# Low part of the rotated keys: from GpSimd at the end of a group to VectorE at the end of the next group's first quad

## The chip, the core and the metric

One core of one Trainium2 chip. The metric is the device time of one execution, in microseconds. A core has TensorE (matrix products into PSUM), VectorE, ScalarE and GpSimd (elementwise work), and queues that issue DMA transfers. VectorE and ScalarE can read PSUM. Each engine runs its own list of instructions in order; semaphores tie the lists together.

## What is computed

Input x is 8 batches of 512 tokens of 256 channels. The output is x + attention(layernorm(x)) + experts(layernorm(x)). The mixture of 16 experts is done before the part that matters here. The attention has 16 heads of 64 channels, with rotated queries and keys and a bias by distance:

```
qkv = (x @ qkv_w.T).reshape(B, S, 3, H, D)
q, k = rope(q, c, s), rope(k, c, s)      # (t1*c - t2*s, t1*s + t2*c)
scores = einsum('bhqd,bhkd->bhqk', q, k) / 8
kb = -p * log1p(a * abs(i - j))
out = einsum('bhqk,bhkd->bhqd', softmax(scores + kb), v)
return out.reshape(B, S, H*D) @ out_w.T
```

## The kernel before

Products of float32 values are made from float16 pairs: a value is split into a high part (its float16 rounding) and a low part (value minus high part, in float16), and each product is three TensorE passes (high-high, high-low, low-high; the list PARTS).

**Stages.** `prepare` (layer norm, routing, tables) and `experts` run first; `attention` takes over at about 280 us of the profile. It has 8 batches of 4 groups; a group is 4 heads of one batch, numbered g = 4b + j. A group has 4 quads, each 128 query rows of all 4 heads; quad n belongs to group n // 4. `over_quads` walks the 128 quads on every engine.

**One quad on TensorE** (`quad`, line 1631): scores (L1572, into four banks ps_s), the transposes of the previous quad's probabilities of two heads (L1585, into ps_t), a fill, the value products of quad n-2 (L1607, first from pt_pe, then from pt_dma), another fill. **Fills** are projections for later groups and the output projection, all through the one PSUM bank ps_x: per group in the order qk0, v0, qk1, v1, qk2, qk3, y0, y1, two to a quad (POSITIONS, line 1026). A fill waits until the one before has been read (`x_free`). The projections (L1528 for q and k, L1538 for v) are for the group F two ahead (`ahead`); the last two groups of batch 7 have none.

**One quad on VectorE** (`quad`, line 1447): read the second fill of the quad before, then `negate` for three heads (L1424: scores scaled plus bias, and their minimum), read this quad's first fill, `negate` for the fourth head, on odd quads `read_context`, and `pair_low` (L1430, low part of the transposed probabilities, out of ps_t). A fill of q or k is read by L1390 (times the cosine and sine table, into prods), one of v by L1374 after ScalarE's L1249. Each of these reads at most one input from SBUF, the other from PSUM.

**ScalarE** does the exponentials (L1286), the high parts (`turned_high` L1270, `prob_high` L1276, `high` L1265 for the rotated queries and keys, at the end of the second and fourth quad of a group), and some copies.

**GpSimd**, per group (`group`, line 1193), in this order: prob_low of the first quad (L1163: low part of the two heads' probabilities that go through a DMA transpose), rotate the queries of F (L1153: sum of products, into rot), ctx_parts (L1171), prob_low of the second quad, multiply (L1143), low part of the rotated queries (`low(F, 0)`, L1157), prob_low of the third, rotate the keys (`rotate(F, 1)`), prob_low of the fourth, **low part of the rotated keys (`low(F, 1)`, L1157)**, ctx_parts, and at the end in batches 0 to 6 either two gathers of expert rows for the next batch (j < 2, L1179, indirect DMAs) or `combine` (j >= 2: L1189 and L1191, which weigh these rows and add them to the residual). The first rotation of the next group waits for the low part of the keys by `parts_lo` >= 2F and by `x_free`.

**The DMA queue** (`turn_probs`) issues the transpose of prob_parts into pt_dma once `prob_lo` of that quad is signalled; the values of that quad wait for it two quads later.

`parts` is a ring of five (high, low) tiles: entry 2F for the queries and 2F + 1 for the keys of group F. The scores of a group wait in their first quad for `parts_lo` >= 2F + 2.

Of the kernel before, what the change touches and what calls it, by code (L numbers as in the profile page):

```python
# [18 lines left out]
ALU = mybir.AluOpType  # L19
# [7 lines left out]
E, F, C = 16, 1024, 256  # L27
TOK = NB * S
NT = TOK // P
TPB = S // P  # L30
KT = M // P
NG, HG = 4, 4
# [947 lines left out]
def attention(nc, sem, ctx, x, out, xt_dram, xcur, x_loaded, o_sb, o_stored, expert_dram, source_dram, gate_dram, ident,  # L980
# [8 lines left out]
    def sb(name, shape, dt=F32):  # L989
        return ctx.enter_context(nc.sbuf_tensor(name, shape, dt))  # L990
# [3 lines left out]
    rot = sb("rot", [P, 2, S])  # L994
    parts = sb("parts", [P, 5, 2, 2, S], F16)
# [53 lines left out]
    parts_hi, parts_lo = sem("parts_hi"), sem("parts_lo")  # L1049
# [9 lines left out]
    def fills_before(b, l):  # L1059

        n = 2 * FILLS + PAIRS * b + l
        n = n - (min(max(l - 6, 0), 2) if b == 0 else 2)
        if b == NB - 1:
            n -= sum(m // 8 >= 2 and m % 8 < FILLS for m in range(l))
        return n
# [5 lines left out]
    def wait(eng, s, v):  # L1071

        if v > 0:
            eng.wait_ge(s, v)

    def ahead(b, j):

        return None if b == NB - 1 and j >= 2 else 4 * b + j + 2
# [59 lines left out]
    def on_gpsimd(pool):  # L1138
        def multiply(F, fills):

            pool.wait_ge(x_free, fills)
            pool.wait_ge(rotated, 2 * F)
            nc.gpsimd.tensor_tensor(prods[:, 0:2, :], proj[:].unsqueeze(1).to_broadcast([P, 2, S]), trig[:, 1:3, :],  # L1143
                                    ALU.mult).then_inc(multiplied, 1)

        def rotate(F, w, fills):

            pool.wait_ge(x_free, fills)
            if w and F >= 2:
                pool.wait_ge(multiplied, F - 1)  # L1150
            pool.wait_ge(parts_lo, 2 * F + w)
            p = prods1 if (F, w) == (1, 1) else prods
            nc.gpsimd.tensor_tensor(rot[:], p[:, 0:2, :], p[:, 2:4, :], ALU.add).then_inc(rotated, 1)  # L1153

        def low(F, w):
            pool.wait_ge(parts_hi, 2 * F + w + 1)
            nc.gpsimd.tensor_tensor(parts[:, (2 * F + w) % 5, 1], rot[:], parts[:, (2 * F + w) % 5, 0], ALU.subtract).then_inc(parts_lo, 1)  # L1157

        def prob_low(n):
            if n < 0 or n == LAST:  # L1160
                return
            pool.wait_ge(prob_hi, n + 1)
            nc.gpsimd.tensor_tensor(prob_parts[:, n % 2, 1], prob[:, (2 * n + 1) % 3], prob_parts[:, n % 2, 0],  # L1163
                                    ALU.subtract).then_inc(prob_lo, 1)

        def context_lo(unit):
            if unit < 0 or unit >= LAST_UNIT - 1:
                return
            two = slice(2 * (unit % 2), 2 * (unit % 2) + 2)
            pool.wait_ge(ctx_hi, unit + 1)  # L1170
            nc.gpsimd.tensor_tensor(ctx_parts[:, 1, two].rearrange("p t c -> p (t c)"), ctxt[:],  # L1171
                                    ctx_parts[:, 0, two].rearrange("p t c -> p (t c)"), ALU.subtract).then_inc(ctx_lo, 1)

        def gather(b, half):

            pool.wait_ge(routes_loaded, 32 * b + 32)
            wait(pool, combined, 2 * b + half - 1)
            for i in range(2 * half, 2 * half + 2):
                nc.gpsimd.indirect_dma_start(  # L1179
                    got[:, i, :], None, expert_dram[:, :],  # L1180
                    bass.IndirectOffsetOnAxis(ap=source[:, i:i + 1], axis=0),
                    bounds_check=E * C - 1, oob_is_err=False).then_inc(gathered[half], 16)

        def combine(b, half):

            pool.wait_ge(gathered[half], 32 * b + 32)
            pool.wait_ge(residual_loaded, 16 * b + 16)
            two = slice(2 * half, 2 * half + 2)
            nc.gpsimd.tensor_tensor(got[:, two, :], got[:, two, :], gate[:, two].unsqueeze(2).to_broadcast([P, 2, M]), ALU.mult).then_inc(weighted, 1)  # L1189
            pool.wait_ge(weighted, 2 * b + half + 1)  # L1190
            nc.gpsimd.tensor_tensor(res[:, two, :], res[:, two, :], got[:, two, :], ALU.add).then_inc(combined, 1)  # L1191

        def group(b, j):
            g = NG * b + j
            F = ahead(b, j)
            prob_low(4 * g)
            if g == 0:
                rotate(1, 1, FIRST_FILLS.index((1, "qk", 3)) + 1)
                combine(0, 0)
                low(1, 1)  # L1200
                combine(0, 1)
            if F:
                rotate(F, 0, fills_before(b, 8 * j) + 3)
            context_lo(2 * g - 1)
            prob_low(4 * g + 1)
            if F:
                multiply(F, fills_before(b, 8 * j) + 5)
            if F:
                low(F, 0)
            prob_low(4 * g + 2)  # L1210
            if F:
                rotate(F, 1, fills_before(b, 8 * j) + 6)
            prob_low(4 * g + 3)
            if F:
                low(F, 1)
            context_lo(2 * g)
            if b < NB - 1:
                if j < 2:
                    gather(b + 1, j)
                else:  # L1220
                    combine(b + 1, j - 2)

        def rotate_queries():

            pool.wait_ge(x_free, 2)
            nc.gpsimd.tensor_tensor(prods0[0][:, 0:2, :], prods0[0][:, 0:2, :], prods0[0][:, 2:4, :], ALU.add).then_inc(rotated, 1)

        rotate_queries()
        for r in range(2):
            pool.wait_ge(o_stored[r], 16 * (E // 2))  # L1230
        gather(0, 0)
        rotate(1, 0, FIRST_FILLS.index((1, "qk", 1)) + 1)
        gather(0, 1)
        low(1, 0)
        for b in range(NB):
            for j in range(NG):
                group(b, j)
# [132 lines left out]
    def on_vector(dve):  # L1370
# [33 lines left out]
        def read_fill(b, l):  # L1404
            kind = fill_at(b, l)
            if kind and kind[0] == "v":
                read_val(kind[2], kind[1])
            elif kind and kind[0] == "qk" and kind[1] != 2:
                dve.wait_ge(filled, fills_before(b, l) + 1)
                read_q(kind[2], kind[1], prods)  # L1410
            elif kind and kind[0] == "y":
                read_y(b, l, kind[1], fills_before(b, l))
# [15 lines left out]
        def pair_low(n):  # L1428
            dve.wait_ge(turned_hi, n + 1)
            nc.vector.scalar_tensor_tensor(out=pt_pe[:, n % 2, 1].rearrange("p q k c -> p q (k c)"), in0=ps_t[:],  # L1430
                                           scalar=P_SCALE, in1=pt_pe[:, n % 2, 0].rearrange("p q k c -> p q (k c)"),
                                           op0=ALU.mult, op1=ALU.subtract).then_inc(turned_lo, 1)

        def read_context(unit):

            dve.wait_ge(pv_done, 4 * unit + 4)
            dve.wait_ge(sums_scaled, unit + 1)
            nc.vector.reciprocal(rsum[:], sums[:, unit % 2].rearrange("p n u -> p (n u)")).then_inc(chain, 1)
            dve.wait_ge(chain, unit + 1)
            if unit == LAST_UNIT:  # L1440
                dve.wait_ge(end_turned, 1)
            else:
                wait(dve, ctx_lo, unit)
            nc.vector.tensor_tensor(ctxt[:].rearrange("p (i d) -> p i d", d=D), ps_o[:].rearrange("p (i d) -> p i d", d=D),
                                    rsum[:].unsqueeze(2).to_broadcast([P, 8, D]), ALU.mult).then_inc(ctx_read, 1)

        def quad(n, b, q):
            j, t = divmod(q, TPB)
            if q:
                read_fill(b, 2 * q - 1)  # L1450
            elif b:
                read_fill(b - 1, PAIRS - 1)
            negate(n, j, t, 0)
            negate(n, j, t, 1)
            negate(n, j, t, 2)
            if n:
                read_fill(b, 2 * q)
            negate(n, j, t, 3)
            if n == 0:
                read_val(0, 1)  # L1460
                read_val(1, 0)
                read_val(1, 1)
                read_q(1, 2, prods1)
                read_q(1, 3, prods1)
                read_fill(b, 2 * q)
            if n % 2 and n >= 3:
                read_context(n // 2 - 1)
            if n:
                pair_low(n - 1)

        def first_low(w):
            dve.wait_ge(parts_hi, w + 1)
# [217 lines left out]
```

## Time and profile before

| | |
|---|---|
| Time, median of three runs | 1146.76 us (1145.97 to 1149.74) |
| Profiled execution | 1150.09 us |
| its span | 1148.4 us |
| TensorE busy | 1064.0 us (93%) |
| ScalarE busy | 1021.2 us (89%) |
| VectorE busy | 1005.8 us (88%) |
| GpSimd busy | 826.6 us (72%) |
| Granted TensorE clock, mean | 0.97 |
| Shares of the chain that ended last | PE 65%, ACT 9%, DMA 8%, DVE 7%, POOL 6%, issue 4% |

The chain is the path of work and waits followed back from the last instruction. PE is TensorE, PEld its weight loads, DVE VectorE, ACT ScalarE, POOL GpSimd. L1157 is line 1157 of the kernel. "Idle before" is the idle time of an engine ahead of an instruction, with what ended it. Instructions of one engine overlap a little at their ends, so that an instruction that waits for nothing starts about 0.08 us before the recorded end of the one ahead of it.

### The profile page before, as it was taken

The page shows a single profiled execution, that of the slowest core. Times are in us where ns is not written, and L with a number is a line of the kernel's source. Part 1 is how long each engine was busy: PE and PEld are TensorE (multiplying, and loading weights), DVE is VectorE, ACT ScalarE, POOL GpSimd, SP SyncE. Part 2 cuts the span into 40 slices and gives each one's busy share as a digit, 9 for nine tenths or more (in the row PEclk, how much of TensorE's full clock was granted, in tenths as well). Part 3 has the DMA queues.
Part 4 walks back from the last instruction along what each step waited for, and adds up shares of the span by engine and source line. Part 5 has one row for each costly group of instructions (what it writes and reads, how often), then busy time and mean ns, then how long its engine had stood idle before and what let it go on. Part 6 is the DMA issues. An engine that isn't in the chain of part 4 may idle for free.

```text
span 1148.4 us, 35585 instructions
## 1 busy us (share of the span) xinstructions
PE 1064.0 (93%) x14470; PEld 776.9 (68%) x14470; DVE 1005.8 (88%) x2050; ACT 1021.2 (89%) x2013; POOL 826.6 (72%) x483
## 2 busy tenths in 40 slices
PE   3547999999799999999999999999999999999977
PEld 2436988887466676676766666767667676776756
DVE  8788999996688999999989888999999988899976
ACT  3797999984589999999999999999999999999985
POOL 5471010002699999899999899989999999999842
PEclk9667999999999999999999999999999999999999
DMA  8885676751148557766766685585667557855564
GB/s 292 311 264 189 208 265 220 240 202 52 33 82 157 113 95 148 130 99 107 167 98 107 130 153 106 95 155 124 101 119 153 112 103 135 153 94 111 112 112 92
DMA packets 383106, 164.75 MB, mean 143 GB/s; under 512 B 336610, under 2 KB 372463, under 8 KB 382944
## 3 DMA queue, kind: packets, MB, share of 16 engines
q1 hardware_dynamic: 368832, 137.98, 57.2%
q0 software_dynamic: 5440, 16.61, 3.9%
q10 hardware_dynamic: 8672, 7.90, 2.3%
q8 instruction: 114, 1.87, 0.7%
q14 instruction: 48, 0.39, 0.1%
HBM read 58.79 MB, written 21.00 MB: 69 GB/s over the span
## 4 chain that ended last, share of the span: by engine, by line
PE 65%; ACT 9%; DMA 8%; DVE 7%; POOL 6%; issue 4%; SPq 0%; POOLq 0%; ACTq 0%; DVEq 0%
PE ps_o L1607 12%; PE ps_s L1572 11%; PE ps_x L1528 10%; PE ps_t L1585 8%; PE ps_x L1547 6%; PE ps_x L1538 6%; PE psh L941 5%; PE pso L956 5%; DMA pt_dma<-prob_parts 4%; ACT prob L1286 2%; DMA ot<-ctx_parts 2%; DVE wlo L874 2%; POOL prob_parts L1163 2%; POOL parts L1157 1%; DMA xt_dram<-xth 1%
## 5 line engine op out<-in xcount | busy, mean ns | idle before, releaser
L1286 ACT ACTIVATE prob<-prob,neg_max 128x512 f32<-128x512 f32 x512 | 365.2, 715 | 4.7 <-DVE neg_max L1424 2.6
L1424 DVE CUSTOM_DVE_ANT_0 prob<-ps_s,strips,score_scale 128x512 f32<-128x512 f32 x512 | 360.4, 746 | 10.3 <-PE ps_s L1572 5.9
L1163 POOL TENSOR_TENSOR prob_parts<-prob,prob_parts 128x1024 f16<-128x1024 f32 x127 | 272.1, 2143 | 78.4 <-ACT prob_parts L1276 78.1
L1572 PE MATMUL ps_s<-parts 32*128 32x512 f16 x3072 | 191.2, 379 | 1.1 <-DVE parts L1473 1.0
L1430 DVE SCALAR_TENSOR_TENSOR pt_pe<-ps_t,pt_pe 128x1024 f16<-128x1024 f32 x128 | 156.0, 1219 | 36.2 <-ACT pt_pe L1270 36.1
L1585 PEld LDWEIGHTS ps_t<-ident,prob 128*128 128x128 f32 x1024 | 110.7, 142 | 58.2 <-issue 38.6
L1153 POOL TENSOR_TENSOR rot<-prods 128x1024 f32<-128x1024 f32 x61 | 144.3, 2365 | 3.2 <-DVE prods L1390 3.2
L1528 PE MATMUL ps_x<-xcur,wqkv_hi 128*128 128x512 f16 x480 | 143.7, 381 | 2.2 <-DVE pt_dma L1390 1.3
L1585 PE MATMUL ps_t<-ident,prob 128*128 128x128 f32 x1024 | 140.7, 281 | 3.8 <-DVE pt_pe L1430 3.8
L771 POOL DMA_DIRECT2D expert_dram<-xa x16 | 17.9, 1120 | 173.1 <-ACT xa L816 173.1
L1276 ACT CAST prob_parts<-prob 128x1024 f16<-128x1024 f32 x127 | 132.9, 1046 | 4.0
L1270 ACT ACTIVATE pt_pe<-ps_t 128x1024 f16<-128x1024 f32 x128 | 130.7, 1021 | 3.8 <-PE ps_t L1585 3.5
L1157 POOL TENSOR_TENSOR parts<-rot,parts 128x1024 f16<-128x1024 f32 x62 | 132.9, 2143 | 0.4 <-ACT parts L1265 0.4
L1572 PEld LDWEIGHTS ps_s<-parts 32*128 32x128 f16 x3072 | 68.9, 93 | 92.5 <-issue 33.4
L1390 DVE TENSOR_TENSOR prods<-ps_x,trig 128x1024 f32<-128x1024 f32 x90 | 110.0, 1222 | 15.8 <-PE ps_x L1528 15.6
L1607 PE MATMUL ps_o<-val_hi,pt_dma 128*128 128x64 f16 x2048 | 111.6, 194 | 11.8 <-DMA pt_dma<-prob_parts 11.7
L1607 PEld LDWEIGHTS ps_o<-val_hi,pt_pe 128*128 128x128 f16 x2048 | 104.0, 98 | 11.0 <-issue 0.3
L1607 PE MATMUL ps_o<-val_hi,pt_pe 128*128 128x64 f16 x2048 | 111.1, 193 | 0.0
L1607 PEld LDWEIGHTS ps_o<-val_hi,pt_dma 128*128 128x128 f16 x2048 | 99.4, 98 | 13.2 <-DMA pt_dma<-prob_parts 6.9
L1607 PE MATMUL ps_o<-val_lo,pt_dma 128*128 128x64 f16 x1024 | 104.1, 194 | 0.0
L1607 PE MATMUL ps_o<-val_lo,pt_pe 128*128 128x64 f16 x1024 | 103.7, 193 | 0.0
L1607 PEld LDWEIGHTS ps_o<-val_lo,pt_pe 128*128 128x128 f16 x1024 | 91.2, 98 | 11.0 <-issue 0.3
(219 smaller groups left out, 2599.4 us busy)
## 6 DMA issues: line engine op xcount, KB each, us to landing
raw<-in_L_ffn_w_dram SPq DMA_DIRECT2D x32, 1024.0 KB, 6.2
xa<-in_L_attn_x_dram SPq DMA_DIRECT2D x8, 512.0 KB, 9.1
slots_dram<-zeros POOLq DMA_DIRECT2D x4, 1024.0 KB, 8.9
xt_dram<-xth SPq DMA_DIRECT2D x8, 512.0 KB, 6.5
xa<-slots_dram SPq DMA_DIRECT2D x16, 256.0 KB, 5.3
expert_dram<-xa POOLq DMA_DIRECT2D x16, 256.0 KB, 5.0
xcur<-xt_dram SPq DMA_DIRECT2D x8, 512.0 KB, 4.8
res<-in_L_attn_x_dram ACTq DMA_DIRECT2D x8, 512.0 KB, 4.1
```

The source lines that it names most:

```text
L1153: nc.gpsimd.tensor_tensor(rot[:], p[:, 0:2, :], p[:, 2:4, :], ALU.add).then_inc(rotated, 1)
L1157: nc.gpsimd.tensor_tensor(parts[:, (2 * F + w) % 5, 1], rot[:], parts[:, (2 * F + w) % 5, 0], ALU.subtract).then_inc(parts_lo, 1)
L1163: nc.gpsimd.tensor_tensor(prob_parts[:, n % 2, 1], prob[:, (2 * n + 1) % 3], prob_parts[:, n % 2, 0], ALU.subtract).then_inc(prob_lo, 1)
L1270: nc.scalar.activation(pt_pe[:, n % 2, 0].rearrange("p q k c -> p q (k c)"), ps_t[:], ACT.Copy, scale=P_SCALE).then_inc(turned_hi, 1)
L1276: nc.scalar.copy(prob_parts[:, n % 2, 0], prob[:, (2 * n + 1) % 3]).then_inc(prob_hi, 1)
L1286: nc.scalar.activation(prob[:, s % 3, q, :], prob[:, s % 3, q, :], ACT.Exp, bias=neg_max[:, 2 * (s % 3) + q:2 * (s % 3) + q + 1], scale=-1 ...
L1424: nc.vector.tensor_tensor_reduce(prob[:, s % 3, q, :], ps_s[u][:], strips[:, HG * j + u, start:start + S], score_scale[:, 0:1], 3.0e38, AL ...
L1430: nc.vector.scalar_tensor_tensor(out=pt_pe[:, n % 2, 1].rearrange("p q k c -> p q (k c)"), in0=ps_t[:], scalar=P_SCALE, in1=pt_pe[:, n % 2 ...
L1528: last = nc.tensor.matmul(bank, wt[a][:, kt, c:c + P], xcur[:, x, kt, :], start=(m == 0), stop=(m == 3 * KT - 1))
L1572: last = nc.tensor.matmul(ps_s[h][:], parts[rows, 2 * F % 5, a, f, t * P:(t + 1) * P], parts[rows, (2 * F + 1) % 5, c, f, :], start=(i == ...
L1585: last = nc.tensor.transpose(ps_t[:, q, kt * P:(kt + 1) * P], prob[:, 2 * n % 3, q, kt * P:(kt + 1) * P], ident[:])
L1607: last = nc.tensor.matmul(ps_o[:, c:c + D], pt[:, n % 2, x, q, kt, :], val[a][:, g, kt, u * D:(u + 1) * D], start=(m == 0), stop=(m == 3 * ...
```

## The change

VectorE gets a function `key_low` with the subtraction that GpSimd's `low(F, 1)` did, with the same operands and semaphores, and runs it at the end of the first quad of each group from the second on (after `pair_low`), for the F of the group before. GpSimd no longer does it in `group`; it still does `low(F, 0)`, and `low(1, 1)` once at the start. 30 operations move, of the groups 0 to 29.

```
@@ group, on GpSimd
             prob_low(4 * g + 3)
-            if F:
-                low(F, 1)
             context_lo(2 * g)
@@ on_vector
+        def key_low(F):
+            dve.wait_ge(parts_hi, 2 * F + 2)
+            nc.vector.tensor_tensor(parts[:, (2 * F + 1) % 5, 1], rot[:], parts[:, (2 * F + 1) % 5, 0], ALU.subtract).then_inc(parts_lo, 1)
@@ quad, on VectorE
             if n:
                 pair_low(n - 1)
+            if n and t == 0 and ahead(*divmod(n // TPB - 1, NG)):
+                key_low(ahead(*divmod(n // TPB - 1, NG)))
```

## Rows read from the trace of the kernel before

**Rows 1.** The page's first part: busy time, share of the span, instructions.
```profile
PE 1064.0 (93%) x14470; PEld 776.9 (68%) x14470; DVE 1005.8 (88%) x2050; ACT 1021.2 (89%) x2013; POOL 826.6 (72%) x483
```
**Rows 2.** Stretch 320 to 1100 us: length, busy time per engine, clock, DMA share, GB/s.
```profile
320.00:1100.00 780.00, 770.83 (x11671) 538.77 (x11668) 702.10 (x1405) 740.98 (x1588) 714.43 (x386) 1.00 0.66 121
```
**Rows 3.** Waits from 320 to 1100 us: total, times, longest.
```profile
POOL prob_parts L1163 <- ACT prob_parts L1276: 54.7, 62, 2.5
...
PE ps_o L1607 <- DMA pt_dma<-prob_parts: 6.0, 10, 1.4
```
**Rows 4.** Timeline of VectorE, quads 64 to 66: start, us, operation, idle before.
```profile
726.58 1.22 DVE L1430 SCALAR_TENSOR_TENSOR pt_pe<-ps_t,pt_pe 128x1024 f16<-128x1024 f32 x1
728.25 0.69 DVE L1374 TENSOR_TENSOR val_lo<-ps_x,val_hi 128x512 f16<-128x512 f32 x1 [0.45 <-ACT val_hi L1249]
728.97 0.75 DVE L1424 CUSTOM_DVE_ANT_0 prob<-ps_s,strips,score_scale 128x512 f32<-128x512 f32 x1
...
730.32 0.75 DVE L1424 CUSTOM_DVE_ANT_0 prob<-ps_s,strips,score_scale 128x512 f32<-128x512 f32 x1
...
731.29 1.23 DVE L1390 TENSOR_TENSOR prods<-ps_x,trig 128x1024 f32<-128x1024 f32 x1 [0.22 <-PE ps_x L1528]
...
733.94 1.22 DVE L1430 SCALAR_TENSOR_TENSOR pt_pe<-ps_t,pt_pe 128x1024 f16<-128x1024 f32 x1
735.07 0.68 DVE L1374 TENSOR_TENSOR val_lo<-ps_x,val_hi 128x512 f16<-128x512 f32 x1
735.67 0.74 DVE L1424 CUSTOM_DVE_ANT_0 prob<-ps_s,strips,score_scale 128x512 f32<-128x512 f32 x1
```
**Rows 5.** Timeline of TensorE, quad 65: its scores, its second fill (v1).
```profile
727.47 1.47 PE L1572 MATMUL ps_s<-parts 32*128 32x512 f16 x24
...
732.58 0.28 PE L1538 MATMUL ps_x<-wqkv_hi,xcur 128*128 128x256 f16 x1
```
**Rows 6.** Timeline of GpSimd over the end of a group that combines.
```profile
725.36 2.15 POOL L1157 TENSOR_TENSOR parts<-rot,parts 128x1024 f16<-128x1024 f32 x1
727.45 1.17 POOL L1171 TENSOR_TENSOR ctx_parts<-ctxt,ctx_parts 128x512 f16<-128x512 f32 x1
...
729.70 1.27 POOL L1191 TENSOR_TENSOR res<-res,got 128x512 f32<-128x512 f32 x1
730.94 2.14 POOL L1163 TENSOR_TENSOR prob_parts<-prob,prob_parts 128x1024 f16<-128x1024 f32 x1
```
**Rows 7.** Timeline of ScalarE, prob_high of quad 64.
```profile
728.96 1.05 ACT L1276 CAST prob_parts<-prob 128x1024 f16<-128x1024 f32 x1
```
**Rows 8.** Timeline of TensorE: waits for a first quad's transposed probabilities.
```profile
345.49 0.19 PE L1607 MATMUL ps_o<-val_hi,pt_dma 128*128 128x64 f16 x1 [0.57 <-DMA pt_dma<-prob_parts]
580.20 0.19 PE L1607 MATMUL ps_o<-val_hi,pt_dma 128*128 128x64 f16 x1 [0.48 <-DMA pt_dma<-prob_parts]
```
**Rows 9.** Timeline of VectorE, first low parts at the start of attention.
```profile
285.21 1.21 DVE L1473 TENSOR_TENSOR parts<-prob,parts 128x1024 f16<-128x1024 f32 x1
286.40 1.23 DVE L1473 TENSOR_TENSOR parts<-pt_pe,parts 128x1024 f16<-128x1024 f32 x1
```
**Rows 10.** Timelines of VectorE and GpSimd where both run side by side.
```profile
2.86 1.02 DVE L449 CAST strips<-strips 128x896 f32<-128x896 int32 x1
2.40 1.00 POOL L286 IOTA pos<- 128x512 int32 x1
...
45.79 0.18 DVE L507 SCALAR_TENSOR_TENSOR col<-col 128x16 f32<-128x16 f32 x1
43.48 2.73 POOL L305 TENSOR_SCALAR xa<-xa,moments,sd 128x256 f32<-128x256 f32 x2 [11.76 <-DVE shift L438]
...
285.43 1.89 POOL L1179 DMA_INDIRECT got<-expert_dram,source  x1 [0.30 <-issue]
```
**Rows 11.** Timeline of GpSimd at the end of a group that gathers.
```profile
648.48 1.16 POOL L1171 TENSOR_TENSOR ctx_parts<-ctxt,ctx_parts 128x512 f16<-128x512 f32 x1
649.79 1.05 POOL L1179 DMA_INDIRECT got<-expert_dram,source  x1
```

## The prediction

> **What bounds the kernel now.** I read the page first: TensorE is busy for 1064.0 of 1148.4 us, VectorE 1005.8, ScalarE 1021.2, GpSimd 826.6 [rows 1]. These are averages over a start, a long steady stage and an end, so the next view is the table by stretches. From 320 to 1100 us TensorE is busy 770.83 of 780 us at full granted clock, VectorE 702.10, ScalarE 740.98, GpSimd 714.43 [rows 2]. All of the moved work lies in or next to this stretch, and in it TensorE is the bound: it can give back at most 9.2 us, whatever is taken from others.
>
> The list of waits says what the 9.2 us are: TensorE's matmuls waited 6.0 us, ten times, for the DMA transpose of the probabilities (pt_dma), which starts when GpSimd's prob_low is done. GpSimd itself waited 54.7 us in all for ScalarE's prob_high [rows 3]. So GpSimd is not late at most of its steps; it is late at some.
>
> Then I laid the engines' timelines of one group boundary side by side (quads 64 and 65, the first two of a group; other regular groups repeat it). On VectorE, pair_low (L1430) starts at 726.58; behind it stand the val_lo read (728.25), the first of the score reads (728.97), the third (730.32) and the read of ps_x into prods (731.29) [rows 4]. That last one ends at 732.52, and TensorE's next projection into the same bank starts at 732.58 [rows 5]: 0.06 us, a bare handoff. ps_x is one bank, so here TensorE waits for VectorE once in this quad, and **every delay of this prods read is a delay of TensorE**, which has nothing else to do in between and no idle time later to win it back.
>
> **What the change removes.** 30 low parts leave GpSimd, one in each of the groups 0 to 29, each 2.15 us beside the one at 725.36 [rows 6]; that is 64 us of GpSimd time. In the group shown, ctx_parts, the two combine operations and prob_low(64) all come 2.1 us earlier until something else holds them. prob_low(64) started at 730.94 right behind the combine [rows 6], while ScalarE's high part for it was done at 728.96 + 1.05 = 730.01 [rows 7]. So it gains 0.9 us, and no more. What follows is rotate, which needs the prods read, and prob_low(65), which already waited for ScalarE. The gain in time is where TensorE waited for the transpose of a first quad's probabilities: 0.57 us at 345.49 and 0.48 us at 580.20 [rows 8]. Together **-1.1 us**; the rest of the 6.0 us stands at other quads, whose prob_low does not move. The moved operation issues no DMA; the gathers and the combine behind it on GpSimd come earlier, and nobody waits for them.
>
> **What it adds, undisturbed.** 30 tensor_tensor on VectorE, 128x1024 f32 and f16 to f16, both inputs in SBUF. The same form exists twice at the start (L1473): 1.21 and 1.23 us, the second 1.19 us behind the first, where the queue was full [rows 9]. pair_low, of the same size, lets its successor start 1.13 us after itself (733.94 to 735.07) [rows 4]. So it takes 1.13 to 1.19 us of the queue, and I take 1.14, near the many.
>
> Where does it go? It would start at 726.58 + 1.13 = 727.71. Its own wait, on parts_hi, is long met (ScalarE makes the high part at the end of the group before). Cover: val_lo could have started at 727.71 and did at 728.25, 0.54 us free; the first score read could follow 0.60 us behind it (735.07 to 735.67), at 728.85, and did at 728.97, 0.12 us; the prods read could follow 0.67 us behind the third score read, at 730.99, and did at 731.29, 0.30 us [rows 4]. That is 0.96 us of cover against 1.14 us, so the prods read is 0.18 us late (0.17 to 0.23). By the handoff above TensorE is late by as much. Regular boundaries are those at quads 8 to 116, 28 of them; the one at quad 4 falls into the irregular start and the one at quad 120 into the end, where ScalarE and the transposes set the pace, and I cost both at nothing (each at most 1.2 us). 28 x 0.18 = **+5.0 us**. Who else waits: the score reads of quad 65 come up to 0.5 us late, and TensorE's next scores overwrite those banks only after the projection at 732.58; ScalarE's shift and prob_low(65) hang on the fourth score read, behind prods, and are late by the same 0.18 as TensorE. On GpSimd the rotate of the next group waited by program order for the low part, and now waits for VectorE; it needs the prods read too, which VectorE does later, so this wait is never the last.
>
> **What it adds, beside GpSimd.** This is the large term. In 14 of the 28 (the second half of batches 0 to 6) the group ends with combine. With the low part gone, its second operation (L1191) starts 2.09 us earlier than 729.70, at 727.61, and runs 1.27 us, to 728.88 [rows 6]. The new VectorE operation wants to start at 727.71, 0.10 us behind it. In the steady stage of the kernel before, every VectorE operation reads one input from PSUM; this is the first with two SBUF inputs beside busy GpSimd. What do rows say of such pairs? At 2.86 a VectorE cast took 1.02 us and ended at 3.88, 0.48 us behind the end of a GpSimd iota that had started before it (2.40 + 1.00) [rows 10]: it was held until GpSimd was done. And a GpSimd indirect DMA that started at 285.43, inside the first L1473, took 1.89 us instead of 1.05 [rows 9 to 11]; L1473 ended at 286.42, and the DMA instruction ended 0.9 us behind that: GpSimd was held by an operation with two SBUF inputs. Against it: L507, with two SBUF inputs but 16 columns, took its usual 0.18 us inside a pair of GpSimd tensor_scalars (43.48 to 46.21) [rows 10]. The first two rows are nearer in size and in what is shared, and I take them: held to 728.88, the operation ends 1.08 us later, its successor starts at 728.88 + 1.00 = 729.88 in place of 728.85, 1.03 us more. The prods read is then 1.21 us late. 14 x 1.21 = 16.9 and 14 x 0.18 = 2.5.
>
> The Trainium skill (SBUF — State Buffer, on the shared port pair) speaks against this change: a VectorE instruction with two SBUF inputs and a GpSimd instruction that reads SBUF share an interface, and whichever starts first has it for its whole length. The rows at 2.86 and 285.43 agree; the row of L507 does not. By that rule the sum is the one just made; without it, the undisturbed one. In the 13 regular groups that end with gathers, these stand where combine stands here: the first starts 1.31 us behind ctx_parts and takes 1.05 [rows 11], so it ends at 725.36 + 2.36 = 727.72, just as VectorE wants to start. The second meets an operation that runs already; GpSimd is held up to 0.9 us, ends near 729.9 and is still ahead of the 730.01 of ScalarE.
>
> **Sum.** 16.9 + 2.5 - 1.1 = +18.3 us. The profiled execution is 1150.09 us (span 1148.4 and 1.7 around it), 3.3 above the median; the terms are differences, and I put them on the median: 1146.8 + 18.3 = **1165 us**.
>
> **The rivals.**
> 1. Held by combine, as above: 1165, 50%.
> 2. No hold, as L507 says, or VectorE comes first after all (the margin is 0.10 us, and an operation may touch memory later than its recorded start): 28 x 0.18 - 1.1 = +3.9, 1151 (1149 to 1153 with the bounds 0.17 and 0.23, and with start and end), 32%.
> 3. They share: VectorE goes at half speed over the 1.17 us of overlap and loses 0.58 us. 14 x 0.58 = 8.1 more, 1159, 13%.
> 4. The other side: GpSimd's 2.1 us are worth more than VectorE's 0.18. The mechanism is the pt_dma wait: transposes issued earlier and at other moments land in time, and all 6.0 us of [rows 3] go. It decides only if the queue time of the new operation is under the cover of 0.96 us, against 1.13 as the shortest row. Then 1146.8 - 6.0 = 1141; with the two moved waits alone, 1146. 5% together, 3% past 0.3%.
> That the change frees GpSimd without anyone profiting is part of all but the last.
>
> **How the numbers follow.** A measurement of this kernel can tell about 0.3% (3.4 us) from no change. Cases 1 and 3 are slower; case 2 lies at +3.9, so a little over half of it is slower and the rest the same; case 4 is faster only where most of the 6.0 us go. Slower 0.50 + 0.13 + 0.17 = 0.80, faster 0.03, same 0.17. The range runs from the lower part of case 2 (1149) to the top of case 1 (28 x 0.05 more for the longer queue time, and start and end): 1168. Outside lie case 4, the foot of case 2 and a tail above. The likeliest case's own range is 1162 to 1168.
>
> **What would show each step.** After: L1157 x32, and 30 of a new VectorE line. Its duration, group by group: 1.21 us in all would kill the large term; about 2.4 us in the 14 boundaries after combine would show it; between, sharing. The L1191 before it: lengthened to about 2.4 us would mean VectorE came first. The start of the v1 projection against the scores of its quad, 5.11 us now (732.58 - 727.47) [rows 5], should be 5.29 in plain groups and 6.3 in held ones. prob_low of first quads should wait for ScalarE in place of running right behind combine. The pt_dma waits at first quads should be gone and the others still there. The prediction is wrong if VectorE's cover is larger than 0.96 us (if val_lo waits for ScalarE longer than now), or if the DMA waits, which are uneven from run to run, change by more than they gain here.

## The result

The changed kernel takes 1160.74 us (median of four runs, 1160.44 to 1163.06); the kernel before takes 1146.67 us in the same measurement. The ratio is 1.0118, with a 95% interval of 1.0102 to 1.0135: 1.2% or 14.1 us slower. The forecast was 1165 us, slower, in a range of 1149 to 1168.

From the page of the changed kernel, its busy times, which answer to [rows 1], and the shares of the chain that ended last:

```profile
PE 1062.3 (92%) x14470; PEld 774.0 (67%) x14470; DVE 1044.5 (90%) x2080; ACT 1021.2 (88%) x2013; POOL 778.9 (67%) x453
...
PE 54%; DVE 23%; ACT 8%; issue 8%; DMA 4%; POOL 3%; SPq 0%; POOLq 0%; DVEq 0%; ACTq 0%
```

VectorE is busy for 38.7 us more and GpSimd for 47.7 us less. VectorE's share of the chain went from 7% to 23%. GpSimd gave up 30 operations of 2.14 us, 64 us, and its busy time fell by only 48: the gathers above all have become longer (L1179 takes 44.7 us in all, 33.7 before). The stretch and the waits from 320 to 1100 us, which answer to [rows 2] and [rows 3] (columns as there):

```profile
320.00:1100.00 780.00, 764.25 (x11504) 531.47 (x11496) 729.72 (x1410) 728.29 (x1560) 658.01 (x351) 1.00 0.65 120
```
```profile
POOL prob_parts L1163 <- ACT prob_parts L1274: 76.5, 87, 3.6
...
POOL rot L1153 <- DVE prods L1388: 27.1, 28, 1.6
...
PEld ps_x L1532 <- DVE val_lo L1372: 10.5, 13, 0.9
...
PE ps_x L1532 <- DVE val_lo L1372: 7.5, 12, 0.7
...
PE ps_x L1542 <- DVE prods L1388: 3.8, 14, 0.3
PE ps_o L1611 <- DMA pt_dma<-prob_parts: 2.7, 5, 0.6
```

TensorE has new waits for VectorE's reads of ps_x, in 12 to 14 places; GpSimd's relief has become waiting time (for ScalarE 54.7 us before, 76.5 us after, and for VectorE's prods 27.1 us). The pt_dma waits read 2.7 us for 6.0, but part of that is the window: the changed kernel is some 12 us later by then, so that its wait of 1.90 us at 1106.23 lies outside, while one of 1.40 us at 1094.08 before lies inside. Between the starts of quads 8 and 120 they are 1.7 us, and 2.9 before. The new operation, line L1434, by its shortest, median and longest duration:

```profile
L1434 DVE TENSOR_TENSOR parts<-rot,parts x30: 1214/1270/2250, 332.0 to 1102.1; 128x1024 f16<-128x1024 f32 x30
```

There are two kinds: 15 of them take 1.21 or 1.22 us, and 13 take 2.15 to 2.25. The two others, at quads 4 and 120, take 1.36 and 1.32 us; each meets the last 0.2 to 0.3 us of a ctx_parts. One of the long ones is at quad 64, behind a group that combines (the same place as [rows 4] and [rows 6]). VectorE and GpSimd:

```profile
730.77 1.22 DVE L1428 SCALAR_TENSOR_TENSOR pt_pe<-ps_t,pt_pe 128x1024 f16<-128x1024 f32 x1
731.91 2.23 DVE L1434 TENSOR_TENSOR parts<-rot,parts 128x1024 f16<-128x1024 f32 x1
734.07 0.68 DVE L1372 TENSOR_TENSOR val_lo<-ps_x,val_hi 128x512 f16<-128x512 f32 x1
...
731.79 1.27 POOL L1191 TENSOR_TENSOR res<-res,got 128x512 f32<-128x512 f32 x1
734.28 2.13 POOL L1163 TENSOR_TENSOR prob_parts<-prob,prob_parts 128x1024 f16<-128x1024 f32 x1 [1.23 <-ACT prob_parts L1274]
```

L1191 starts at 731.79 and ends at 733.06. L1434 starts 0.12 us behind it, lasts 2.23 us and ends at 734.14, 1.08 us behind the end of L1191. Undisturbed it takes 1.22 us, so all of it but some 0.14 us came after GpSimd's end. L1191 itself kept its 1.27 us. Engines that shared would show about 1.8 us here, by the prediction's third rival. TensorE in the quad behind it, where the bracket is the idle time:

```profile
731.66 1.47 PE L1576 MATMUL ps_s<-parts 32*128 32x512 f16 x24
...
734.80 0.60 PE L1532 MATMUL ps_x<-xcur,wqkv_hi 128*128 128x512 f16 x2 [0.64 <-DVE val_lo L1372]
...
737.95 0.28 PE L1542 MATMUL ps_x<-wqkv_hi,xcur 128*128 128x256 f16 x1 [0.28 <-DVE prods L1388]
```

The v1 projection starts 6.29 us after the quad's scores; it was 5.11 in [rows 5]. At quad 68, behind a group that gathers:

```profile
759.00 1.22 DVE L1434 TENSOR_TENSOR parts<-rot,parts 128x1024 f16<-128x1024 f32 x1
760.14 0.68 DVE L1372 TENSOR_TENSOR val_lo<-ps_x,val_hi 128x512 f16<-128x512 f32 x1
...
757.96 1.04 POOL L1179 DMA_INDIRECT got<-expert_dram,source  x1 [0.15 <-issue]
759.31 1.78 POOL L1179 DMA_INDIRECT got<-expert_dram,source  x1 [0.31 <-issue]
```

Here VectorE's operation takes 1.22 us, and the second gather, which starts inside it, takes 1.78 us in place of 1.0: it is GpSimd that waits.

I took the length of a quad as the distance from its first scores to the next quad's. In the 28 second quads of the regular stretch (after quads 8 to 116) it was 6.52 or 6.53 us before. After, it is 6.68 us in 14 of them, 6.52 us in one, and longer in 13 (7.62 to 7.71 us, once 7.02). Together that is 16.5 us. The other quads between 8 and 120 gave back 2.7 us. Of the 14 places behind combine, one is not long, at quad 96:

```profile
944.60 1.22 DVE L1434 TENSOR_TENSOR parts<-rot,parts 128x1024 f16<-128x1024 f32 x1
...
944.61 2.35 POOL L1191 TENSOR_TENSOR res<-res,got 128x512 f32<-128x512 f32 x1
```

VectorE came first by 0.01 us, and GpSimd's operation was long instead, 2.35 us for 1.27. That quad takes 6.68 us.

### The profile page after: what moved, and what is told of

Read it like the earlier page. It is cut to its first block, busy times and chain, and to the rows that moved or that the text cites. A ratio compares the mean times of both kernels' runs of the same rounds, so it can differ in the third digit from the quotient of the medians.

```text
span 1158.6 us, 35585 instructions
## 1 busy us (share of the span) xinstructions
PE 1062.3 (92%) x14470; PEld 774.0 (67%) x14470; DVE 1044.5 (90%) x2080; ACT 1021.2 (88%) x2013; POOL 778.9 (67%) x453
## 4 chain that ended last, share of the span: by engine, by line
PE 54%; DVE 23%; ACT 8%; issue 8%; DMA 4%; POOL 3%; SPq 0%; POOLq 0%; DVEq 0%; ACTq 0%
PE ps_s L1576 10%; PE ps_x L1532 9%; PE ps_t L1589 7%; PE ps_o L1611 7%; PE ps_x L1551 6%; DVE prods L1388 6%; PE pso L956 5%; DVE prob L1422 5%; PE psh L941 5%; PE ps_x L1542 3%; DVE pt_pe L1428 3%; DMA pt_dma<-prob_parts 2%; DVE wlo L874 2%; ACT prob L1284 2%; DVE parts L1434 1%
## 5 line engine op out<-in xcount | busy, mean ns | idle before, releaser
L1542 PE MATMUL ps_x<-wqkv_hi,xcur 128*128 128x256 f16 x496 | 91.9, 274 | 7.5 <-DVE prods L1388 6.5
```

## The experiments

They ran on three chips (0, 15 and 4). On all of them the stages before attention take over 20 us longer than in the first measurement (the first scores of the changed kernel start at 286.3 us there and at 311.3 us in its second profile), while the quads have the same lengths. Ratios are against the kernel before on the same chip. The theory: VectorE's new operation is held by a running GpSimd instruction because it reads two SBUF inputs, and that is where most of the 14 us go. The rivals: the operation or its place is slow for another reason; VectorE's load as such costs the time; or GpSimd's relief is worth more or less than thought.

**The change again.**

> The changed kernel once more, beside the three above. Expected as measured before, 1.0118 times the kernel before, with about 13 of 30 operations of 2.2 us.

Measured: 1186.1 us, ratio 1.0116 (1.0097 to 1.0136). The regular stretch from quad 8 to quad 120 takes 744.9 us in both profiles of the change, and again 13 of the 30 operations take 2.16 to 2.25 us. The loss carries over.

**Combine moved ahead of ctx_parts.**

```
             prob_low(4 * g + 3)
+            if b < NB - 1 and j >= 2:
+                combine(b + 1, j - 2)
             context_lo(2 * g)
...                                    # and no combine behind it; gather stays here
```

> The changed kernel, but in groups that combine GpSimd does combine ahead of ctx_parts in place of behind it. Nothing is added or left out. Theory (VectorE's new operation, with two SBUF inputs, is held until the GpSimd instruction that runs already is done): the second combine operation now ends within 0.05 us of the start of the new operation, so this lasts at most 1.3 us in the 13 or 14 places where it lasted 2.2, the quads behind it take 6.7 us in place of 7.7, and the time falls by 13 x 1.0 to about 1148 us. ctx_parts starts at the same moment as the new operation; should GpSimd be first there, VectorE is held again and the time stays near 1161; the trace tells which. Rival (the long ones are long for another reason, such as what VectorE does at these places): 2.2 us remain wherever combine has moved, and about 1161 us.

Measured: 1182.7 us, ratio 1.0079 (1.0056 to 1.0102). This fell between the two expected times, and the trace shows why: L1171 (ctx_parts) now starts within 0.1 us of VectorE's operation, in most places within 0.01, and half of the 14 places go one way and half the other. Quads 44 and 48:

```profile
622.54 1.22 DVE L1433 TENSOR_TENSOR parts<-rot,parts 128x1024 f16<-128x1024 f32 x1
...
622.54 2.24 POOL L1171 TENSOR_TENSOR ctx_parts<-ctxt,ctx_parts 128x512 f16<-128x512 f32 x1
...
648.62 2.23 DVE L1433 TENSOR_TENSOR parts<-rot,parts 128x1024 f16<-128x1024 f32 x1
...
648.62 1.16 POOL L1171 TENSOR_TENSOR ctx_parts<-ctxt,ctx_parts 128x512 f16<-128x512 f32 x1
```

In 7 places GpSimd is held (its operation takes 2.15 to 2.25 us for 1.16), in 7 VectorE (2.19 to 2.23 us for 1.22). Never both, and never neither. It is not combine's operands that matter: ctx_parts does the same.

**The operation ahead of pair_low, with two SBUF inputs and with one.**

```
+            if n and t == 0 and ahead(...):
+                key_low(...)          # second kernel: reads ps_t in place of rot
             if n:
                 pair_low(n - 1)
-            if n and t == 0 and ahead(...):
-                key_low(...)
```

> The changed kernel, but the new VectorE operation stands ahead of pair_low in place of behind it, 1.13 us earlier. Theory (held): it now starts about 0.1 us behind the first combine operation (L1189, 1.05 us) and is held by that one: about 2.1 us long in the groups that combine, 1.2 in the others, and the quads behind the long ones take about 7.5 us; 1157 to 1159 us. Rival (it is the second combine operation alone, by its operands, that matters): 1.2 us everywhere and 6.7 us quads.

> As ahead_of_pair, at the same place and of the same shape, but the first input is the PSUM tile ps_t in place of rot in SBUF, so that the operation has one SBUF input. (The low part of the rotated keys is left out; the values are others.) Theory (two SBUF inputs are what lets GpSimd hold it): 1.22 us in all 30 places, also inside the first combine operation, quads of 6.7 us, about 1148 us. Rival (any VectorE operation at this place beside GpSimd's combine is slowed, or the held time comes from memory and not from the count of SBUF inputs): still about 2.1 us in 14 places, 1157 us or more.

The second kernel leaves the low part of the rotated keys out, and its operation also waits for the transposed probabilities in ps_t, as pair_low does. Measured, one run each: 1184.2 us and 1176.7 us, against 1173.2 for the kernel before (ratios 1.009 and 1.003, without an interval). The durations decide. First the kernel with rot, then the one with ps_t, each behind the group before quad 64, with the GpSimd instructions beside it:

```profile
754.03 2.03 DVE L1434 TENSOR_TENSOR parts<-rot,parts 128x1024 f16<-128x1024 f32 x1
...
753.93 1.05 POOL L1189 TENSOR_TENSOR got<-got,gate_now 128x512 f32<-128x512 f32 x1
755.06 2.13 POOL L1191 TENSOR_TENSOR res<-res,got 128x512 f32<-128x512 f32 x1
```
```profile
750.78 1.22 DVE L1435 TENSOR_TENSOR parts<-ps_t,parts 128x1024 f16<-128x1024 f32 x1
...
750.68 1.04 POOL L1189 TENSOR_TENSOR got<-got,gate_now 128x512 f32<-128x512 f32 x1
751.81 1.27 POOL L1191 TENSOR_TENSOR res<-res,got 128x512 f32<-128x512 f32 x1
```

With rot, VectorE waits for L1189 and then runs; L1191, which comes while it runs, waits for VectorE (2.13 for 1.27 us). So it is in 13 of the 14 places behind a combine, and the quads behind them take 7.4 to 7.5 us (once 6.84), as expected. With ps_t both engines run side by side at full speed. Over all 30 places of that kernel:

```profile
L1435 DVE TENSOR_TENSOR parts<-ps_t,parts x30: 1216/1220/1226, 356.1 to 1115.9; 128x1024 f16<-128x1024 f32 x30
```

Same place, same shape, same neighbours; only the second SBUF input is gone, and with it the hold, in both directions. **This settles the cause of the long ones.** It agrees with the rule of the Trainium skill (SBUF — State Buffer, on the shared port pair) that was weighed in the prediction, and nearly so in its "whole instruction": VectorE's held operation ends 1.07 to 1.09 us behind the end of the one that held it, whether 0.3 or 1.15 us of that one were left, so that only its first 0.13 to 0.14 us ran beside the other.

The time of the kernel with ps_t is 3.5 us above the kernel before, where the theory gave 1.3, and its trace shows where that lies. The quads behind groups that combine take 6.68 us (one 6.53). Those behind groups that gather grew to between 6.59 and 7.06 us in 13 places: the gathers come earlier there and nothing holds them. The cost of such early gathers is the subject of three experiments below.

**Only the groups that do not combine.**

```
+            if F and b < NB - 1 and j >= 2:      # GpSimd, ahead of context_lo
+                low(F, 1)
```

and the opposite condition at VectorE's `key_low`.

> Half of the change: VectorE makes the low part of the keys only for the 16 groups that do not combine; in the 14 that combine GpSimd makes it as in the kernel before. Theory (held by combine): all 16 operations last 1.21 to 1.3 us, their quads take 6.68 us against 6.53, 16 x 0.15 = 2.4 us are added and at most 1 us comes back: 1148 us. Rival (each moved operation costs the same, whatever GpSimd does): 14.1 x 16 / 30 = 7.5 us are added: 1154 us.

Measured: 1172.9 us, ratio 0.9990 (0.9979 to 1.0001); no change that can be told, and a little less than the 1.3 us more that the theory gave. The operations in the regular stretch take 1.22 us and their quads 6.68 us (6.52 or 6.60 in three, each behind a quad that was longer itself, two of those by a wait for pt_dma). The rival's 7.5 us are excluded.

**All groups, but GpSimd's combine out of the way.**

```
+            if b < NB - 1 and j >= 2:
+                combine(b + 1, j - 2)
             prob_low(4 * g + 3)
             context_lo(2 * g)
...                                    # and no combine behind it; gather stays here
```

> The changed kernel, but GpSimd does combine ahead of prob_low of the fourth quad, where it waited 1.1 us for ScalarE; nothing is left out. ctx_parts then ends near 727.69 in the time of the group shown, just ahead of VectorE's 727.71. Theory (held only by a GpSimd instruction that runs): no place above 1.3 us, all quads behind the new operation 6.68 us, 28 x 0.15 = 4.2 us added and 1 to 3 us given back: within 0.3% of the kernel before. Rival (the loss is VectorE's load as such): as the changed kernel, 1.2% more.

Measured: 1173.2 us, ratio 1.0010 (0.9997 to 1.0023). VectorE does the same 30 operations as in the change, and the 1.2% are gone. Its operation over all places, and the place of the group shown:

```profile
L1433 DVE TENSOR_TENSOR parts<-rot,parts x30: 1212/1214/1377, 355.0 to 1114.1; 128x1024 f16<-128x1024 f32 x30
```
```profile
747.66 1.16 POOL L1171 TENSOR_TENSOR ctx_parts<-ctxt,ctx_parts 128x512 f16<-128x512 f32 x1
...
748.79 1.21 DVE L1433 TENSOR_TENSOR parts<-rot,parts 128x1024 f16<-128x1024 f32 x1
```

ctx_parts ends at 748.82 by the record, 0.03 us into VectorE's operation, and does not hold it. Most quads behind the operation take 6.68 us; two are longer (7.36 and 7.17), because TensorE waits in them for pt_dma (0.75 and 0.56 us); three are shorter (6.52 to 6.54). This is the second rival of the prediction (no hold) made true, by a change of order: +1.2 us, with an interval of -0.4 to +2.7 us, which is less than the 3.9 us that the prediction gave it. VectorE's load as such is not the loss.

**GpSimd's relief alone.** GpSimd does 16 of the 1024 columns, VectorE nothing.

```
-                low(F, 1)
+                low_sliver(F)         # the same, columns 0:8 of both halves
```

> The kernel before, but GpSimd's low part of the rotated keys covers 16 of 1024 columns (the rest of it is left out), and VectorE gets nothing: what GpSimd's 2 us per group are worth alone. The prediction's step says 1.1 us (0.1%); the difference left over by the other terms (17.4 added by VectorE, 14.1 measured) says 3.3 us (0.3%), by fewer waits of TensorE for pt_dma at all quads. A rival that GpSimd is the true bound would give 10 us or more.

Measured: 1173.7 us against 1172.1, ratio 1.0013 (1.0000 to 1.0026). I expected 1 to 3 us less; it is not faster at all. The pt_dma waits did shrink (to 1.2 us between quads 8 and 120, from 2.9 in the kernel before), but 13 second quads, all behind groups that gather, grew by 0.1 to 0.6 us. One of them, TensorE's scores, VectorE and GpSimd:

```profile
459.79 1.47 PE L1577 MATMUL ps_s<-parts 32*128 32x512 f16 x24
...
460.57 0.69 DVE L1379 TENSOR_TENSOR val_lo<-ps_x,val_hi 128x512 f16<-128x512 f32 x1 [0.45 <-ACT val_hi L1254]
462.25 0.75 DVE L1429 CUSTOM_DVE_ANT_0 prob<-ps_s,strips,score_scale 128x512 f32<-128x512 f32 x1 [0.98 <-PE ps_s L1577]
...
459.15 1.04 POOL L1184 DMA_INDIRECT got<-expert_dram,source  x1
460.49 1.00 POOL L1184 DMA_INDIRECT got<-expert_dram,source  x1 [0.30 <-issue]
```

VectorE waits 0.98 us for the scores of the quad, although the record has the scores at their usual 1.47 us. The trace's semaphore events show TensorE's signal of them 2.43 us after their start in this quad and 1.48 us in a quad behind combine; in all 13 quads it is 0.43 to 0.95 us late. In the kernel before and in the change no signal of scores in the regular stretch is late. In the kernel with ps_t above it is late in the same 13 quads (0.06 to 0.84 us).

**Is it the moment of the gathers?** The kernel before with the order of GpSimd's last steps changed in the 14 groups that gather; nothing left out.

```
+            if b < NB - 1 and j < 2:
+                context_lo(2 * g)
+                gather(b + 1, j)
+                low(F, 1)
...                                    # else: the order of before
```

> The kernel before, but in the 14 groups that gather, GpSimd does ctx_parts and the two gathers ahead of the low part of the keys, so that the gathers start 2.1 us earlier; nothing is removed, and VectorE gets nothing. Theory (gathers at this earlier moment delay the signal of the scores of the next second quad, as in relief_only): in 13 quads the signal comes 0.4 to 0.9 us late, these quads take 6.8 to 7.1 us in place of 6.53, and the kernel is 4 to 6 us (0.4%) slower than before. Rival (the late signals of relief_only come from the missing GpSimd work, not from the gathers' moment): no late signal and no change.

Measured: 1176.9 us against 1174.0, ratio 1.0027 (1.0013 to 1.0041). The signal of the scores is late in the same 13 quads, by 0.27 to 0.85 us, of which up to 0.5 us reach the length of the quad. So it is the moment of the gathers and not the missing work. The loss is smaller than the 4 to 6 us expected (about 3, between 1.5 and 4.8). Which part of a gather does it, its instruction or its transfer, stays open.

**Relief without moving a gather.** The sliver only in the 14 groups that combine.

```
+            if F and b < NB - 1 and j >= 2:
+                low_sliver(F)
+            elif F:
                 low(F, 1)
```

> The kernel before, but in the 14 groups that combine GpSimd's low part of the keys covers 16 of 1024 columns (the rest of it is left out); the groups that gather are untouched, so that no gather moves. Theory (GpSimd's time is worth something only through TensorE's waits for pt_dma, and relief_only lost it again through its gathers): no late signals, no longer quads, and 0 to 2 us (up to 0.2%) less than the kernel before. Rival (GpSimd's time is worth 3 us per 30 groups as the difference between my terms and the measurement says): 1.5 us less.

Measured: 1172.3 us against 1174.0, ratio 0.9989 (0.9976 to 1.0002), no late signal of scores. But "no longer quads" failed: four second quads behind groups that gather, which this edit leaves alone, took 6.79 to 7.02 us. In three of them (quads 9, 57 and 89) it is the signal of the first fill that comes 0.27 to 0.41 us late, with the gathers where they stand in the kernel before. What GpSimd's time is worth is 0 to 3 us for these 14 groups; a size within that is not to be had.

**Half the work, where no GpSimd tensor operation stands beside it.**

```
+            if F and combines(b, j):   # b < NB - 1 and j >= 2
                 low(F, 1)
+            elif F:
+                low_half(F)            # GpSimd: first half; VectorE's key_low: second
```

> In the 16 groups that do not combine, GpSimd makes one half of the low part of the keys (512 columns) and VectorE the other, at the place of the change; in the 14 that combine GpSimd makes all, as before. Theory (VectorE has 0.96 us of cover before the prods read, and no GpSimd instruction to be held by): the half takes about 0.6 us of the queue, is covered whole, the quads behind it stay at 6.53 us, and the time is that of the kernel before or up to 2 us less. Rival (the cover is an artefact and every VectorE addition costs TensorE in proportion): 6.6 us quads and 1 us more.

Measured: 1175.7 us against 1172.1, ratio 1.0027 (1.0011 to 1.0042). A miss in the time, though the cover was right. Where VectorE's half is undisturbed:

```profile
383.68 0.68 DVE L1451 TENSOR_TENSOR parts<-rot,parts 128x512 f16<-128x512 f32 x1
384.27 0.69 DVE L1387 TENSOR_TENSOR val_lo<-ps_x,val_hi 128x512 f16<-128x512 f32 x1
```

It takes 0.59 us of the queue and the quad stays at 6.53 us. But a half no longer holds the gathers for long, in five places not at all, and in exactly these five the signal of the scores is late (0.52 to 0.82 us); four of the quads take 7.0 us and the fifth 6.77. Together that is 2.3 us of second quads; the rest of the 3.5 us I can't place.

No version tried beats the kernel before by more than its interval.

## Why the prediction was right, point by point

**The bound and the handoff: right.** TensorE has no spare time, and a late read of ps_x is a late TensorE. The v1 projection was forecast at 6.3 us after its scores in held quads and came at 6.29 in the one shown. One thing I had not followed: the late val_lo holds the first fill of the quad too (the 0.64 us above), ahead of the prods read. It changes nothing in the sum, since the same lateness is passed on once.

**The undisturbed cost: right, 0.15 us per boundary for 0.18.** The operation takes 1.13 to 1.14 us of the queue, the lower end of what was given, so the cover is 0.98 us for the 0.96 that was read. The half operation, 0.59 us, was covered whole, which agrees.

**The hold: right in mechanism, place and size.** 2.23 us for a forecast of about 2.3, in 13 of 14 places, up to 1.18 us per quad for 1.21. The time alone does not show it: 1160.7 us lies below the likeliest case's own range of 1162 to 1168 and nearer to the third rival's 1159. The durations do: 2.23 us is no sharing, and L1191 lost nothing. A lead of 0.10 to 0.19 us decided it each time, and once, at quad 96, VectorE came first. That the order held so often was a forecast from a margin of 0.10 us, and in part luck. Of the two witnesses only the row at 285.43 was one for two SBUF inputs; at 2.86 VectorE's cast had one input and GpSimd's iota read nothing, and no run takes that row up. The row of L507 against it (16 columns inside a GpSimd instruction) proved to be no guide; why so small an operation slips through was not tried.

**The sum of these terms was too large by 3 us.** Forecast 16.9 + 2.5 = 19.4, found 16.5 in the regular stretch: one hold fewer (1.0), 13 holds a little shorter, plain boundaries at 0.15 and one at nothing, and one held quad of only 7.02 us, behind a quad in which TensorE had waited for pt_dma anyway.

**The relief: direction right, size not resolved.** The pt_dma waits at first quads' probabilities are gone as forecast (1.1 us). The quads between 8 and 120 that are not second ones gave back 2.7 us. Their pt_dma waits fell by 1.2 us, 0.5 of it at the first-quad wait of 580.20 [rows 8] already counted, and TensorE's weight loads waited 0.4 us for the transposed context (ot) in place of 1.6, a term that the prediction does not have. Such waits are uneven, and one profile of each kernel does not tell how much of this is the change. With the 3 us above, it is why +14 came out and not +18. The stretch of quads 8 to 120 went from 731.1 to 744.9 us, +13.8, which is what the medians say (+14.1). The two profiled executions differ by less, 10.3 us, because the profiled execution of before was 3.4 us above its median.

**The gathers: this step was wrong in its reason.** I wrote that the gathers come earlier and nobody waits for them. The experiments show that gathers about 2 us earlier cost about 3 us in all (1.5 to 4.8), through late signals of TensorE. In the changed kernel they start as early, and no signal of scores is late; there VectorE's new operation holds the second gather for 0.8 us. The pair with rot and with ps_t points to the hold as the reason: with ps_t no gather is held and 13 signals are late, with rot the gathers are held in 12 of these places and the one late signal is behind quad 104, where one is not. So two effects that I had both priced at nothing cancel, and that the forecast did not suffer from it was luck.

## What to carry to other kernels

Before elementwise work moves from GpSimd to VectorE, look at where its inputs lie: here an operation of this size with two SBUF inputs and GpSimd's elementwise instructions took turns, each for nearly its whole length, and the duration from an idle moment (1.22 us) told nothing of that price. Lay both engines' timelines side by side with the moved work taken out, since its removal shifts what stands beside it; here a 0.1 us order decided 1 us each time. If such a move is wanted, move GpSimd's neighbour first: with combine in an idle slot, the same change cost nothing that could be measured.

## What the runs showed of the hardware that was not expected

The turn-taking is sharp: starts within 0.01 us of each other go either way, but from a lead of 0.02 us on the first always had its way (so VectorE at quad 96 of `ahead_of_pair`, where L1189 took 2.09 us for 1.04). The one that loses is longer by what is left of the other less 0.12 to 0.18 us: VectorE by 1.01 us when 1.15 were left and by 0.14 when 0.29 were left, L1191 by 1.08 when 1.21 were left; with 0.03 to 0.06 us left VectorE is not held at all (`combine_early`). An indirect DMA instruction of GpSimd also waits for such an operation (about 1.8 us for 1.0). It does not where the two start within 0.04 us of each other: there the DMA instruction took its usual 1.04 us, and VectorE's operation 0.03 to 0.07 us more (five places of `half_gather`, one of `ahead_of_pair`). Nor does VectorE seem to wait for one that runs already: in the kernel before, an operation of 512 columns with two SBUF inputs (L470) took 0.68 us at 75.66 us, 0.33 us into one of 0.97, and 0.69 us elsewhere.

Where two unheld gathers started 0.6 to 0.9 us before and 0.5 to 0.7 us after the scores of a quad, TensorE's signal of these scores came late, mostly by 0.3 to 0.95 us (13 quads in each of three kernels: `relief_only`, `gather_sooner` and `ahead_of_pair_psum`); quad 101 is the odd one, with both some 0.4 to 0.7 us earlier. In the five places of `half_gather` they started about 0.3 and 1.6 us after the scores (quad 101 again earlier). Started 1.2 and 2.6 us after the scores, as in the kernel before, they did not delay it, but in `relief_combine_groups` the signal of the next fill was late in three of these quads. What links them is open.
